# One-hot tiles of the scatter matmuls and of the inverse tables laid out token first

## The reference, cut to what matters

```python
# layer 0, mixer: mixture of experts, top 2 of 8 (needs an inverse table slot -> token)
# layer 0, ffn (PEER): 4096 expert rows on a 64 x 64 grid, top 8 of both key halves, 8 heads
sim = einsum("pbnhd,hkpd->pbnhk", q, keys)
...
idx = take_along_axis(ix * 64 + iy, pk)                # 8 heads x 8 picks per token
o = gelu(einsum("bnd,bnhkd->bnhk", inputs, key_in[idx])) * softmax(scores)
y = einsum("bnhk,bnhkd->bnd", o, key_out[idx])
# layer 1, mixer: an LSTM over 256 steps, 16 sequences
# layer 1, ffn: attention, then a mixture of experts, top 2 of 8 (a second inverse table)
```

## Time and profile before

| | |
|---|---|
| Three runs | 3323.02, 3327.69 and 3328.48 us, median 3327.69 |
| The profiled execution | 3329.2 us, its span 3327.3 us |
| TensorE busy | 3090.9 us, 93% of the span, 28718 matmuls |
| VectorE busy | 1934.7 us, 58% |
| ScalarE busy | 1190.9 us, 36% |
| GpSimd busy | 491.6 us, 15% |
| Mean granted TensorE clock | 0.959 of full speed |

### The profile page before, as it was taken

One profiled execution on the slowest core, in us unless ns is written; L12 is line 12 of the kernel. 1 busy time (PEld: TensorE's weight loads), 2 busy tenths in 40 slices (PEclk: granted clock), 3 DMA queues, 4 the chain that ended last, 5 costly groups with the idle time before them and its releaser, 6 DMA issues.

```text
span 3327.3 us, 72707 instructions
## 1 busy us (share of the span) xinstructions
PE 3090.9 (93%) x28718; PEld 2424.8 (73%) x28718; DVE 1934.7 (58%) x6645; ACT 1190.9 (36%) x2696; POOL 491.6 (15%) x645
## 2 busy tenths in 40 slices
PE   7999969999999999999999999966999957999997
PEld 5578558777777777777777777634666645999996
DVE  3245457666666666666666666534676735444443
ACT  0133222333333333333333333222555532555553
POOL 0366000000000000000000000002234321333332
PEclk9999969999999999999999999977999987999998
DMA  3122430101010110101010101110122112222223
GB/s 131 43 87 88 144 137 5 33 18 33 17 33 24 27 30 21 30 21 33 17 33 17 33 18 33 32 47 1 56 83 77 43 54 82 39 36 39 36 39 77
DMA packets 89666, 153.50 MB, mean 46 GB/s; under 512 B 17152, under 2 KB 72192, under 8 KB 86176
## 3 DMA queue, kind: packets, MB, share of 16 engines
q1 hardware_dynamic: 68736, 111.50, 11.8%
q0 software_dynamic: 20448, 37.32, 5.3%
q10 hardware_dynamic: 144, 0.03, 0.0%
HBM read 100.53 MB, written 52.46 MB: 46 GB/s over the span
## 4 chain that ended last, share of the span: by engine, by line
PE 75%; DVE 5%; DMA 2%; ACT 2%; issue 1%; SPq 1%; POOL 0%; POOLq 0%; DVEq 0%; ACTq 0%
PE ps L847 14%; PE ps L670 13%; PE ps L830 8%; PE ps L908 8%; PE ps L1807 8%; PE ps L1822 7%; PE ps L881 3%; PE ps L698 2%; PE ps L699 2%; PE ps L1217 1%; PE ps L1321 1%; PE ps L1277 1%; PE ps L1342 1%; PE ps L1393 1%; PE ps L1254 1%
## 5 line engine op out<-in xcount | busy, mean ns | idle before, releaser
L670 PEld LDWEIGHTS ps<-arena 128*128 128x128 f32 x4096 | 536.8, 192 | 29.7 <-issue 2.5
L847 PE MATMUL ps<-arena 128*128 128x256 f32 x2048 | 551.7, 393 | 0.0
L670 PE MATMUL ps<-arena 128*128 128x128 f32 x4096 | 539.6, 276 | 2.0 <-ACT arena L678 2.0
L847 PEld LDWEIGHTS ps<-arena 128*128 128x128 f32 x2048 | 355.5, 190 | 161.5 <-issue 132.5
L678 ACT ACTIVATE arena<-ps 128x256 f32<-128x256 f32 x512 | 193.2, 384 | 525.8 <-PE ps L670 524.9
L929 DVE SCALAR_TENSOR_TENSOR arena<-arena 128x128 f32<-128x128 f32 x256 | 74.1, 289 | 442.1 <-ACT arena L920 442.0
L908 PE MATMUL ps<-arena 128*16 128x256 f32 x4096 | 283.1, 396 | 29.1 <-DVE arena L938 28.7
L830 PE MATMUL ps<-arena 64*128 64x32 f16 x8192 | 296.7, 245 | 1.5 <-DVE arena L818 1.5
L830 PEld LDWEIGHTS ps<-arena 64*128 64x128 f16 x8192 | 277.2, 158 | 17.9 <-DVE arena L818 2.4
L920 ACT ACTIVATE arena<-ps 128x256 f32<-128x256 f32 x256 | 97.8, 382 | 532.1 <-PE ps L908 532.1
L1549 POOL MEMSET arena<- 128x3072 f32 x1 | 2.7, 2658 | 1845.4 <-PE ps L847 1845.4
(11 more groups left out here) (272 smaller groups left out, 4768.1 us busy)
## 6 DMA issues: line engine op xcount, KB each, us to landing
xw_scratch<-arena SPq DMA_DIRECT2D x32, 512.0 KB, 2.6
arena<-xw_scratch SPq DMA_DIRECT2D x128, 128.0 KB, 4.1
arena<-in_W SPq DMA_DIRECT2D x16, 1024.0 KB, 5.2
arena<-ys_scratch SPq DMA_DIRECT2D x16, 512.0 KB, 8.7
x_scratch<-arena SPq DMA_DIRECT2D x64, 128.0 KB, 2.2
xn_scratch<-arena SPq DMA_DIRECT2D x32, 129.0 KB, 2.7
arena<-in_xT SPq DMA_DIRECT2D x8, 512.0 KB, 8.1
arena<-in_kinT SPq DMA_DIRECT2D x1, 4096.0 KB, 14.6
```

The lines of the kernel that those rows point to most:

```text
L670: m = e.matmul(bank(b)[:, 128 * i:128 * i + 128], kin[:, k, 2 * jp + i, :], xcT[:, k, 128 * blk:128 * blk + 128], start=(k == 0), stop=(k ...
L847: m = e.matmul(bank(7)[:, 0:256], G[blk % 2][:, j, :], kout[:, j, :], start=(j == 0), stop=(j == 31))
```

## The change

X, both Y, `oh` and `bk` are laid out token first, `[p, 16, 128]` and so on, so that the matrix of one token is contiguous for the weight load and for the moving read. To write them in that order, VectorE repeats the counting row over the 16 tokens (a middle dimension with step 0) and each token's number along the row (the innermost dimension with step 0). Before, the counting table `iot` held every number 16 times (512 KB), and the token's number was repeated along the middle dimension; now `iok` holds each number once (32 KB). All matmuls, their number, their order and their results stay as they are.

```diff
-        iot, cw, pcol = take(128, 16, dt=f16), take(4, 16, dt=f16), take(1)
+        cw, pcol = take(4, 16, dt=f16), take(1)
+        iok = take(128, dt=f16)
...
# invert_vector
-            e.tensor_tensor(bk[:, g, 0], iot[:, 0:72], bf[:, 1, 16 * g:16 * g + 16].unsqueeze(1).to_broadcast([128, 72, 16]),
-                            ALU.is_equal).then_inc(iv, 1)
-            e.tensor_tensor(oh[:, g], iot, bf[:, 0, 16 * g:16 * g + 16].unsqueeze(1).to_broadcast([128, 128, 16]), ALU.is_equal)
+            e.tensor_tensor(bk[:, g, :, 0], iok[:, 0:72].unsqueeze(1).to_broadcast([128, 16, 72]),
+                            bf[:, 1, 16 * g:16 * g + 16].unsqueeze(2).to_broadcast([128, 16, 72]), ALU.is_equal).then_inc(iv, 1)
+            e.tensor_tensor(oh[:, g], iok.unsqueeze(1).to_broadcast([128, 16, 128]),
+                            bf[:, 0, 16 * g:16 * g + 16].unsqueeze(2).to_broadcast([128, 16, 128]), ALU.is_equal)
...
-            e.tensor_tensor(bk[:, g, 1], bk[:, g, 0], cw[:, g].unsqueeze(1).to_broadcast([128, 72, 16]), ALU.mult
+            e.tensor_tensor(bk[:, g, :, 1], bk[:, g, :, 0], cw[:, g].unsqueeze(2).to_broadcast([128, 16, 72]), ALU.mult
...
-            e.tensor_scalar(bk[:, g, 0], bk[:, g, 0], pcol, None, ALU.mult).then_inc(iv, 1)
+            e.tensor_scalar(bk[:, g, :, 0], bk[:, g, :, 0], pcol, None, ALU.mult).then_inc(iv, 1)
# invert_tensor
-                m = e.matmul(bank(b)[:, 0:144], oh[:, g, :, c], bk[:, g].rearrange("p v n c -> p (v n) c")[:, :, c],
+                m = e.matmul(bank(b)[:, 0:144], oh[:, g, c], bk[:, g, c].rearrange("p v n -> p (v n)"),
...
-        X = [take(128, 16, dt=f16) for _ in range(2)]
-        Y12 = [take(2, 32, 16, dt=f16) for _ in range(2)]
+        X = [take(16, 128, dt=f16) for _ in range(2)]
+        Y12 = [take(2, 16, 32, dt=f16) for _ in range(2)]
...
# onehot_vector
-            e.tensor_tensor(Y12[b][:, 1], iot[:, 0:32], R16[:, 1, t0:t0 + 16].unsqueeze(1).to_broadcast([128, 32, 16]),
-                            ALU.is_equal).then_inc(s["xy"], 1)
-            e.tensor_tensor(X[b], iot, R16[:, 0, t0:t0 + 16].unsqueeze(1).to_broadcast([128, 128, 16]), ALU.is_equal)
+            e.tensor_tensor(Y12[b][:, 1], iok[:, 0:32].unsqueeze(1).to_broadcast([128, 16, 32]),
+                            R16[:, 1, t0:t0 + 16].unsqueeze(2).to_broadcast([128, 16, 32]), ALU.is_equal).then_inc(s["xy"], 1)
+            e.tensor_tensor(X[b], iok.unsqueeze(1).to_broadcast([128, 16, 128]),
+                            R16[:, 0, t0:t0 + 16].unsqueeze(2).to_broadcast([128, 16, 128]), ALU.is_equal)
...
-            e.tensor_tensor(Y12[b][:, 0], Y12[b][:, 1], R16[:, 2, t0:t0 + 16].unsqueeze(1).to_broadcast([128, 32, 16]),
+            e.tensor_tensor(Y12[b][:, 0], Y12[b][:, 1], R16[:, 2, t0:t0 + 16].unsqueeze(2).to_broadcast([128, 16, 32]),
...
-            e.tensor_tensor(Y12[b][:, 1], Y12[b][:, 1], R16[:, 3, t0:t0 + 16].unsqueeze(1).to_broadcast([128, 32, 16]),
+            e.tensor_tensor(Y12[b][:, 1], Y12[b][:, 1], R16[:, 3, t0:t0 + 16].unsqueeze(2).to_broadcast([128, 16, 32]),
...
# wgroup_tensor
-                        m = e.matmul(bank(4 + half)[:, 32 * q:32 * q + 32], X[b][p0:p0 + 64, :, q],
-                                     Y12[b][p0:p0 + 64, i, :, q], start=(i == 0), stop=(i == 1))
+                        m = e.matmul(bank(4 + half)[:, 32 * q:32 * q + 32], X[b][p0:p0 + 64, q],
+                                     Y12[b][p0:p0 + 64, i, q], start=(i == 0), stop=(i == 1))
```

More of the change, by code:

```diff
@@ L211, in build @@
         axs = [axs_[:, i] for i in range(NXA)]
-        a_oh = take_at(after_a + 8192, 4, 128, 16, dt=f16)
-        a_bk = take_at(after_a + 16384 + 14 * 256, 4 * 2 * 72 * 16, dt=f16).rearrange("p (g v n c) -> p g v n c", g=4, v=2, n=72)
+        a_oh = take_at(after_a + 8192, 4, 16, 128, dt=f16)
+        a_bk = take_at(after_a + 16384 + 14 * 256, 4 * 2 * 72 * 16, dt=f16).rearrange("p (g c v n) -> p g c v n", g=4, v=2, n=72)
         arena.at = base
@@ L552, in moe1_sync @@
             e.dma_start(i72, I["iota72"]).then_inc(s["tri"], 16)
-            e.dma_start(iot, I["iota128"]).then_inc(s["ivc"], 16)
+            e.dma_start(iok, I["iotaK"]).then_inc(s["ivc"], 16)
             e.dma_start(cw, I["cw"]).then_inc(s["ivc"], 16)
@@ L1739, in build @@
         q_bu, q_bf, q_w = take(2, 64, dt=u32), take(2, 64, dt=f16), take(3, 72)
-        q_oh, q_bk = take(4, 128, 16, dt=f16), take(4 * 2 * 72 * 16, dt=f16).rearrange("p (g v n c) -> p g v n c", g=4, v=2, n=72)
+        q_oh, q_bk = take(4, 16, 128, dt=f16), take(4 * 2 * 72 * 16, dt=f16).rearrange("p (g c v n) -> p g c v n", g=4, v=2, n=72)
         assert arena.at <= WORDS - 16384
@@ L2088, in layout @@
         "iota8": np.tile(np.arange(8, dtype=np.float32), (128, 1)),
-        "iota128": np.ascontiguousarray(np.broadcast_to(np.arange(128, dtype=np.float16)[None, :, None], (128, 128, 16))),
+        "iotaK": np.ascontiguousarray(np.broadcast_to(np.arange(128, dtype=np.float16)[None, :], (128, 128))),
         "half": half,
```

## The result

The changed kernel takes 3218.35 us (median of four runs, 3216.57 to 3223.69) against 3327.43 for the kernel before (four runs, 3323.02 to 3328.48): a ratio of 0.968, 95% interval 0.966 to 0.969. The profiled execution took 3216.57 us, its span 3214.7 us. The time is inside the range of 3198 to 3290, 20 us under the forecast of 3238.

A forecast was written before the change was run, and what follows sets the result against it. TensorE was taken to bound the expert-lookup and recurrence stage. Loop -93, first block +4.5, first table -6 and second table +3 sum to -91.5 us, from 3329.2 to 3238 us; range 3198 to 3290.

The forecast's parts named there:

- What bounds the kernel: Expert-lookup and recurrence stage: TensorE busy 640 of 640 us; time taken out of scatter matmul L830 shortens the stage.
- The strided read: Scatter and inverse-table matmuls: elements 32 bytes apart cost 1.88 ns a column; a strided load is 35 such reads.
- TensorE's price per pair: Scatter matmul after the change: 32 ns a pair, at most 1.04 us saved a group; 0.85 us taken.
- c = 1.9 us: VectorE's one-hot compares and products: added cost a group from the innermost repeat, at L127's rate; range 0 to 3.3.
- The chains: VectorE's in-order queue and DMA round trip in the loop: a stall of 0.25 us, 0.4 us a block charged.
- if L908 waits more than 1 us a block: Listed sign that the prediction is wrong: the recurrence matmul's waits in the loop exceed 1 us a block.
- signs listed: Expected after: L830 at 18 to 22 ns a matmul, groups 1.2 to 1.6 us from L908, loads near 110 ns.
- First block and tables: Stage's first block +4.5 us; first inverse table, ahead of the stage, about -6 us; second table +3 us.
- (1): Rival: TensorE's issue limits scatter half-way, some 14 ns an instruction, group 1.8 us; 3275 us, chance 0.13.
- (2): Rival: issue already limits the scatter at 17.5 ns, saving 0 in L830; 3331 us, no change, chance 0.08.
- (3): Rival: VectorE keeps two elements a cycle in the one-hot lines, no stall; 3209 us, chance 0.09.
- (4): Rival: VectorE's one-hot lines at L720's rate, c = 3.3, use up TensorE's gain; slower, 3344 us, chance 0.10.

The follow-up runs named there:

- run with pairs: Changed kernel with each token's number and weight stored twice, so VectorE's innermost repeat is a pair: 3138.78 us, ratio 0.943 to the kernel before.
- reads alone: Kernel before, VectorE untouched, scatter matmul reading contiguous stretches of the old layout for both operands: 3199.24 us, ratio 0.950.
- writes alone: Kernel before, VectorE writing the scatter's one-hot tiles token first, matmuls still reading with a stride of 16: 3390.3 us, ratio 1.007.

## Why the prediction was right, and what it mis-sized

- **What bounds the kernel: right.** Time taken out of L830 came out of the stage: 5.4 us a block where VectorE's work was left alone.
- **The strided read: right.** 1.88 ns a column explained both sorts of matmul. The reading of the load, 32 to 35 reads of that length, is borne out by the run with only Y contiguous, where a pair stays at 62 ns. The contiguous load came out shorter than forecast, 93 ns for 110.
- **TensorE's price per pair: the mis-sized term.** The prediction said "32 x 0.87 + 4 = 32 ns a pair", which is a saving of 1.04 us a group, and took 0.85. Measured: 25 ns a pair and 1.34 us a group. The 1.04 was worked out from a rate called "the upper price", so it was the least that the read could save; the prediction then used it as the most, with zero as the other end, and the truth lay outside both. Two assumptions on the rate failed as well. The rate of 0.87 ns a column came from f32 passes, and f16 columns are faster: the 16 matmuls of 144 columns in the L173 stretch at 72.35 start 62.5 ns apart, 0.43 ns a column, half the f32 rate's time. And at 32 columns the columns don't set the pair's 25 ns, since 8 in every second pair left it the same. The load's estimate of 27 ns was nearer to that, but no run shows that the load sets it.
- **VectorE: right.** c = 1.9 us was forecast from L127's one element in 1.054 ns; measured (2281 - 1217) + (679 - 413) + (683 - 419) + (692 - 425) ns = 1.86 us. The rule of the Trainium skill (Vector Engine (DVE) Microarchitecture Reference, section Performance modes), one element a cycle for a two-source op with 2-byte operands of which one is a single element read again and again, agrees with the trace: 512 f16 elements took 679 ns and 2048 took 2281, 1.04 ns an element, where it was 0.52. The run with pairs shows the way around it, which the prediction did not see.
- **The chains: right in place, too small in size.** In the block shown L911 stands at +19.45 for a predicted 19.5 and L941 is done at +26.7 for 26.9. But the average of that L911 is +19.9, because the DMA round trip varies, and TensorE would be there at +18.75, not at 19.3. So L911 waits 1.1 us a block, and with L850 behind L860, which was in no term, about 1.5 us, instead of 0.4. By the prediction's own list that is a sign of being wrong ("if L908 waits more than 1 us a block"): the place of the wait was right, its charge was not.
- **Luck in the total.** TensorE saved 5.4 us a block where 3.4 were forecast, and the waits took 1.6 where 0.4 were. The two misses pull opposite ways and leave 3.8 us net against 3.0; the first alone would have put the time some 60 us under the forecast. Three more of the signs listed came out beyond their bounds: 14 ns a matmul for 18 to 22, groups of 0.90 us for 1.2 to 1.6, loads of 93 ns for 110.
- **First block and tables:** +5.9 for +4.5; the second table +3.3 for +3; the start -9.5 for -6, of which the table's stretches are 6.5 and the higher clock behind them 2.8, which was in no term. The 3.3 us more from the last scatter group to the last recurrence step and the 3.3 us less in attention were in no term either. The first of these takes 104.8 to 112.0 us over the kernels, and 110.1 in "reads alone", with VectorE untouched, so its change can't be put down to VectorE's longer lines. Attention took 393.0 to 395.0 us in the profiles of the other twelve kernels, whatever was edited; so the 396.9 of the kernel before is the one that stands out.
- **The sum:** -21.2 us in the 30 blocks, -3.5 at the start and -0.6 at the end; against them +1.4 (first block), +2.7 (last block) and +0.3 (second table), with the +3.3 and -3.3 cancelling: 21 us between -91.5 and -112.6.
- **The rivals.** (1) and (2), a limit by issue: a group would have stayed at 1.8 or 2.24 us; it takes 0.90, or 128 instructions at 7 ns each. The 25 ns of the Trainium skill (TensorE: Matmul & The Clock Gate, section Wait — 56ns, not 53.3ns?) as the least distance of two matmuls would make a group 1.78 us, an estimate, if it held for all 64 in turn, and the trace speaks against that. The two halves of the rows run side by side: the starts are 3 and 22 ns apart in turn, 25 ns a pair, so the trace agrees with the Trainium skill for each half alone. (3), VectorE keeps its rate: 2281 ns speak against it; the run with pairs gives that case, at 3139 us. (4), c = 3.3: c was 1.86.
- **Where the method was thin.** The prediction let a loss begin, with no gain for TensorE, only from c = 2.8, by the sum of one block's passes; its own chain through the round trip leaves 20.1 - 17.6 = 2.5. In the run with the writes alone it began below 1.86, at 0.3 us a block, because that chain had 0.6 us of room and the round trip varies by more (8.8 to 11.2 us). The prediction took the round trip from one block, a quick one. Even with its own saving of 0.85 us the average of +19.9 would have meant a wait of some 0.6 us at this step, an estimate, and not 0.25.

## What to carry to other kernels

A load and a moving read that are both strided run side by side, so changing only one of them brings less than a fifth of the gain (0.24 and 0.14 of 1.29 us a group here): change both, and don't price the new rate by rows of another type. When a layout moves the repeat of a VectorE operand to the innermost dimension, store the repeated value twice and repeat the pair: the double rate stays. When a hidden engine gets slower, look first at what its queue puts behind the longer work: a store with a DMA round trip behind it is late by all of it, however much idle time the engine has. Read such a round trip over many blocks: its slow ones set the loss.

## What the runs showed of the hardware

- A pair of 64-row matmuls on the two halves of the rows, each with its own load of 128 f16 columns, took 25 ns (64 of them 0.792 us from first to last start), with 32 moving columns or with 8 in every second pair. With the load or the columns 32 bytes apart it took 60 to 62 ns, with both 66.
- A moving column 32 bytes behind the last one cost 1.88 ns at 1.2 GHz and at a mean clock of 0.75; contiguous, 16 matmuls of 144 f16 columns took 1.16 us in the first table and 2.10 us in the second, starts 62.5 and 120 ns apart, so there the clock does matter.
- The granted clock fell during strided matmuls though TensorE was no less busy: from 66 to 130 us it was busy for 62.44 us both with strided tables (before) and with contiguous ones (pairs), at a mean clock of 0.87 and of 1.00. Contiguous reads don't keep it up by themselves: the group at 76.52 us, after 3.0 us of waiting, fell to 1.2 GHz within four matmuls (1.98 us for 16, against 1.16).
- The same DMA round trip, from the store's issue to the seed's start, took 8.8 to 11.2 us from block to block in "writes alone".
- A VectorE compare of 2048 f16 elements took 1217 ns with a whole row of 16 of one operand repeated, 2281 ns with one element repeated, and 1214 ns with a pair repeated.
